# A graph network's weight tables: part of the low-weight multiplication moved from VectorE to GpSimd

## The reference

```
src, dst = sorted by dst                        # 103125 edges
# layer 0, ten times
agg = segment_sum((h * norm_src)[src], dst)     # counts of edges
h = 0.9 * (agg * norm_dst) + 0.1 * h0
# layer 1, three times, w = edge_weight
norm = dinv[src] * w * dinv[dst]
out = segment_sum((h @ W)[src] * norm, dst)     # weights of edges
```

## Time and profile before

| | |
|---|---|
| Median of three runs | 3808.62 us (3804.43 to 3809.42) |
| The profiled execution | 3773.04 us, span 3771.2 us |
| Mean granted TensorE clock over the span | 0.845 of full |
| PE busy over the span | 2851.2 us, 76% |
| DVE | 1979.1 us, 52% |
| ACT | 1593.7 us, 42% |
| POOL | 1698.0 us, 45% |

### The profile page before, as it was taken

The page is one execution under the profiler, slowest core; times in us unless marked ns, Lnnn a source line. Parts: engine busy times, 40 slices in busy tenths (PEclk is TensorE's granted clock), DMA queues, the critical chain, the costliest instruction groups (busy, mean ns, idle before and its releaser), DMA issues. The chain is left out here.

```text
span 3771.2 us, 69211 instructions
## 1 busy us (share of the span) xinstructions
PE 2851.2 (76%) x17480; PEld 1934.9 (51%) x17480; DVE 1979.1 (52%) x6941; ACT 1593.7 (42%) x4621; POOL 1698.0 (45%) x1766
## 2 busy tenths in 40 slices
PE   2777777999968857777777777778857777777778
PEld 2666654555534425566656566657734443434436
DVE  6999985666631444444444444446844444444443
ACT  1888871333300013333333333334634444444446
POOL 2222211444400046666666666663056666766660
PEclk6999999999989967777787877778868888889885
DMA  1222222556699922222222222222022222222220
GB/s 32 89 90 90 90 82 67 188 196 205 209 380 381 366 65 54 56 55 56 55 55 56 56 55 56 55 57 51 21 58 65 64 65 65 68 64 66 64 61 17
DMA packets 417669, 369.96 MB, mean 98 GB/s; under 512 B 175609, under 2 KB 342233, under 8 KB 417337
## 3 DMA queue, kind: packets, MB, share of 16 engines
q1 hardware_dynamic: 365912, 315.65, 25.7%
q0 software_dynamic: 46144, 48.98, 6.7%
q10 hardware_dynamic: 5280, 1.23, 0.1%
HBM read 279.65 MB, written 86.00 MB: 97 GB/s over the span
## 5 line engine op out<-in xcount | busy, mean ns | idle before, releaser
L1469 POOL DMA_INDIRECT big<-row_table,src x806 | 762.6, 946 | 459.1 <-issue 186.5
L1888 POOL DMA_INDIRECT big<-message_table,src x610 | 623.8, 1023 | 378.6 <-issue 167.8
L1494 PE MATMUL banks<-big 97*128 x902 | 398.1, 532 | 287.1 <-issue 269.2
L1576 DVE SCALAR_TENSOR_TENSOR big<-big,banks 128x97 f32 x451 | 142.6, 316 | 531.1 <-PE banks L1510 292.8
L505 PE MATMUL banks<-work 128*128 128x226 f16 x1197 | 312.3, 261 | 105.1 <-ACT banks L536 43.6
L1927 PE MATMUL banks<-big 128*128 128x512 f16 x1225 | 378.6, 425 | 5.1 <-DVE big L2006 5.1
L1510 PE MATMUL banks<-big 128*128 x1804 | 336.7, 320 | 38.6 <-issue 26.0
L869 PE MATMUL banks<-big,work 128*128 128x512 f16 (+1 forms) x1750 | 345.5, 355 | 17.0 <-DVE work L1006 17.0
L1521 ACT COPY big<-banks 97x256 f32<-97x256 f32 x403 | 148.1, 368 | 486.6 <-remote 270.0
L1494 PEld LDWEIGHTS banks<-big 97*128 97x128 f32 x902 | 173.4, 239 | 343.8 <-issue 339.8
L1510 PEld LDWEIGHTS banks<-big 128*128 128x128 f32 x1804 | 309.9, 243 | 49.7 <-issue 48.9
(11 more groups left out here) (339 smaller groups left out, 5701.2 us busy)
## 6 DMA issues: line engine op xcount, KB each, us to landing
big<-weights_halves SPq DMA_DIRECT2D x16, 6400.0 KB, 20.8
weights_dense<-work SPq DMA_DIRECT2D x196, 200.0 KB, 1.9
work<-weights_dense SPq DMA_DIRECT2D x196, 200.0 KB, 2.8
weights_halves<-work SPq DMA_DIRECT2D x98, 400.0 KB, 2.6
big<-q_table SPq DMA_DIRECT2D x451, 64.0 KB
big<-in_ef SPq DMA_DIRECT2D x403, 64.0 KB
big<-in_ea SPq DMA_DIRECT2D x403, 32.0 KB
big<-row_table,src POOLq DMA_INDIRECT x806
```

Of the source, the lines that this page charges most:

```text
L1469: po.indirect_dma_start(rows[:, t % RT, s, 0:D], None, x_t.rearrange("a p c -> (a p) c"), bass.IndirectOffsetOnAxis(ap=m.src2[:, s, t:t + ...
L1494: pe.matmul(psS[v % 2], qT[v % R][0:XW, :], XF[0:XW, bass.ds(slot, 1), :].rearrange("p t e -> p (t e)"), start=False, stop=True).then_inc( ...
L1888: po.indirect_dma_start(G[n % R][:, s, :], None, g_t.rearrange("a p c -> (a p) c"), bass.IndirectOffsetOnAxis(ap=m.src2[:, s, t:t + 1], ax ...
```

## The change

A new function `low_parts` on POOL multiplies the rows of the last four visits of a batch (LOWS = 6, so visits 6 to 9) by the low weights: 512 elements a partition. It waits until DVE has made the batch's rows (`rows_ready`) and adds one to a semaphore of its own, `lo_ready`. DVE multiplies only visits 0 to 5, 768 elements. PE waits for `lo_ready` before visit 6. POOL's copy for batch b waits for `lo_ready` of batch b - 2 besides, since it overwrites what that multiplication reads.

```diff
+        lo_ready = sem("build_lo")
...
+        LOWS = TP - 4
+        pairwise = lambda a: a.rearrange("p t (r u) -> p t r u", u=2)
+
+        def low_parts(po, b):
+
+            rows = slots[b % 2][0]
+            po.wait_ge(rows_ready, b + 1)
+            value = twice[b % 2][:, WLO, LOWS:TP, :].unsqueeze(2).to_broadcast([P, TP - LOWS, P // 2, 2])
+            po.tensor_tensor(pairwise(rows[:, 2, LOWS:TP, :]), pairwise(rows[:, 0, LOWS:TP, :]), value, ALU.mult).then_inc(lo_ready, 1)
+
         @block.gpsimd
         def _(po):
             for b in range(NBATCH):
                 if b >= 2:
                     po.wait_ge(oh_ready, b - 1)
+                    po.wait_ge(lo_ready, b - 1)
                 po.tensor_copy(twice[b % 2], m.tabs5()[:, :, b * TP:(b + 1) * TP].unsqueeze(3).to_broadcast([P, 5, TP, 2])).then_inc(doubled, 1)
+                if b >= 1:
+                    low_parts(po, b - 1)
+            low_parts(po, NBATCH - 1)
...
                 dve.wait_ge(rows_ready, b + 1)
-                for i, kind in ((1, WHI), (2, WLO)):
-                    ins = dve.tensor_tensor(pairwise(rows[:, i, :, :]), pairwise(rows[:, 0, :, :]), value(kind, P), ALU.mult)
-                ins.then_inc(oh_ready, 1)
+                dve.tensor_tensor(pairwise(rows[:, 1, :, :]), pairwise(rows[:, 0, :, :]), value(WHI, P), ALU.mult)
+                low = twice[k][:, WLO, 0:LOWS, :].unsqueeze(2).to_broadcast([P, LOWS, P // 2, 2])
+                dve.tensor_tensor(pairwise(rows[:, 2, 0:LOWS, :]), pairwise(rows[:, 0, 0:LOWS, :]), low, ALU.mult).then_inc(oh_ready, 1)
...
                 for t in range(min(TP, V0 - b * TP)):
+                    if t == LOWS:
+                        pe.wait_ge(lo_ready, b + 1)
                     if t % GV == 0:
                         pe.wait_ge(freed, needed[t // GV] & 255)
```

## The result

The changed kernel takes 3852.59 us (median of four runs, 3841.55 to 3858.78) against 3806.52 us (four runs, 3802.95 to 3809.42): ratio 1.0116, 95% interval [1.0101, 1.0132], 46 us slower. The forecast was 3889 us, slower, in a range from 3840 to 3945. The direction and the mechanism of steps 1 to 3 came as forecast; the size is a little over half of the 80 us, and the mechanism of step 4 did not occur.

The account below looks back on a forecast made before the run. PE, at 3.80 us a batch, bounds the table stage, with DVE close behind at 3.52. 119 x (4.45 - 3.80) = 77 us plus 3 us once gives 3808.6 + 80 = 3889 us; own range 3865 to 3915, outer 3840 to 3945.

Parts of the forecast that it names:

- steps 1 to 3: Table stage: DVE saves 0.27 us a batch, POOL's 1.19 us multiplication holds DVE 1.0 us; DVE's batch becomes 4.32 us.
- step 4: Table stage: POOL's multiplication doesn't get in until PE and DVE stop; 4.48 us a batch, up to 4.58; 4.45 taken.
- Step 1: DVE's second multiplication in the table stage loses 512 of 1280 elements: 0.27 us less, DVE's own work 3.25 us a batch.
- Steps 2 and 3: POOL's added table-stage multiplication takes 1.19 us a batch and, getting in ahead of L468, costs DVE 1.0 us.
- step 3: Table stage: POOL's multiplication holds DVE for 1.0 us a batch, its 1.19 us less 0.20.
- The sign that I had named: In the new profile's table stage, the last start of L481, the former L466, near 617 us.
- Step 6: Start of the table stage: POOL's configuration instruction ahead of its first multiplication costs 3 us once, between 0 and 8.
- Rival A: PE's clock falls in the table stage too: 0.35 us a batch more, 42 us, 3931 us; chance 0.17.
- Rival B: Table stage: POOL holds DVE only for elements read, at the copy's rate; 3.68 us a batch, 3809 us; chance 0.06.
- Rival C: Table stage: POOL and DVE run side by side, PE's sequencer ends the gain at 12 us, 3797 us; chance 0.05.
- Rival D: Table stage: DVE is stopped only 0.6 to 0.8 us a batch, about 30 us, 3839 us; chance 0.06.

Follow-up runs that it names:

- the saving alone: Changed kernel with the low weights of the last four visits multiplied by nobody from the third batch on: 3394.65 us against 3406.93 before; with one-batch legs 3403.74 us.
- the memset: Changed kernel with POOL setting the same 512 elements to zero instead of multiplying them: 3395.34 us against 3407.66 before, ratio 0.9965.
- before with legs of one: Kernel before, with PE reading 12 registers ahead of each batch instead of 24 ahead of every second: 3405.01 us against 3407.66, ratio 0.9990.

## Why the prediction was right

**What bounds the stage.** Right for the direction: DVE and PE both near 3.8 us, DVE with something to spare. Wrong in one point that didn't reach the sum: I took the pace of before as the larger of two numbers, 3.52 with small waits and 3.80. The table shows a blend, with PE's floor at 3.72. Above 4 us the blend is gone, so the distance to 4.17 us was not hurt by it.

**Step 1, the saving.** 0.27 us a batch predicted, 0.735 - 0.46 = 0.27 measured.

**Steps 2 and 3, the price.** The mechanism was right and was read from the right rows: two instructions that read SBUF take turns, and POOL gets in ahead of L468. The size was off. The multiplication lasts 1.03 us alone, not 1.19, because it costs 1.67 ns an element and not the 2.18 ns of the operations in the earlier trace rows. Those have f32 operands; no run shows whether that is the reason. Taking off 0.20 us for the start was right (0.18 us), so the hold is 0.85 us, not 1.0.

**Step 4, the form in which POOL is shut out.** This is the term whose mechanism did not come. I took DVE's 16 waits for POOL in the earlier trace rows for its count and let it pull the batch from 4.32 to 4.45 us. The count was read wrongly: of the 120 copies of before only ten take over 3 us, and others of those waits stand beside a copy of 0.27 us that ran while DVE was idle already (the wait at 193.28 us, with a copy at 192.89, is one). POOL was not shut out in one of the 118 batches: the longest multiplication is 1.992 us, 1.03 plus the wait for L482. In the traces a copy was shut out for a whole batch in before (3.59 us) and in three kernels in which POOL likewise reads nothing but its copies (the saving alone with either leg, and the memset, 3.32 us in each); in all the kernels in which POOL also multiplies or copies rows, and in before with legs of one, the longest copy is under 1 us. What decides it stays open; the moment of asking alone does not, since in the earlier trace rows the copy that was shut out and the one that got in both asked about 0.15 us after the start of an L466. My price of step 4, 4.48 us, was thus never tested.

**The sum.** With the two terms as measured, 3.25 + 0.85 + 0.07 = 4.17 us, (4.17 - 3.80) x 119 = 44 us, and 3 us once: 47 us, against 46 and 47 measured. Of the 33 us too much, 119 x 0.15 = 18 us come from step 3, the larger part, and 119 x 0.13 = 15 us from step 4. The sign that I had named, the last L481 near 617 us, was missed for the same reason (582.7 us); L483 over 1 us and POOL's multiplication far over 1.2 us in the median (1.99) came.

**Step 6, once.** 3 us predicted, 2.85 us of PE and 3.1 us of DVE measured; the configuration lay 7.0 us ahead.

**Rival A, the clock.** Out: 1.00 from 100 to 500 us, at a PE share of 281.64 / 400 = 70%. The stretch at 69% and 0.80 in the earlier trace rows was no guide to this stage. With eight visits on POOL, at 4.8 us a batch, the same stretch has PE busy for 64% and a clock of 0.97; there too the stage is the sum of DVE's steps and its waits at the start.

**Rival B** had the right sign of its doubt: its price per element read, 0.07 us for 100, is close to what was found, 0.08. It missed that a multiplication reads two operands. 512 x 2 x 0.7 ns would have been 0.72 us. This was the better way to the number than the duration of a different operation.

**Rival C** gave 12 us for the saving at no price, which is what the two kernels with legs of two gained in which POOL reads nothing but its copies. Its premise was wrong, its ceiling right.

**Rival D**, a hold of 0.6 to 0.8 us and 30 us in all, lay as near to the result as the forecast's own range did from the other side. I gave it 0.06, and the range from 3865 to 3915 us missed the result by 12 us; only the outer range held it, and only because it reached down to D. That the time lay inside is as much the width of that range as the sum.

## What to carry to other kernels

Before moving work from DVE to POOL, look for one POOL instruction beside DVE's two-input ones in the trace: if it lasts longer there than alone, count the elements that POOL would read, take the price of each from the neighbour's stretched duration, and compare with what DVE saves on an element. Here it was 1.66 ns against 0.52, so none of the splits run here won, and where DVE sets the pace each element moved loses. Only the work that POOL wrote without reading was free. Where two engines of nearly the same pace pass work through two slots and one of them has an uneven load, a small addition to the other need not be hidden: here 0.2 us a batch on DVE, under PE's pace, cost 8 us.

## What the runs showed of the hardware that was not expected

- A DVE instruction with two SBUF operands was held 0.81 ns for each element that a POOL instruction read: 0.41 us for one operand of 512 and 0.85 us for two. All operands were f16. A POOL memset of 512 elements beside them held it not at all.
- The hold is shown in the duration of the DVE instruction that starts next: a compare of 260 elements, 0.28 us by itself, showed 1.98 us.
- PE's load of registers from SBUF took 0.86 us for 12 and 1.85 us for 24, with the array idle. Half as many at a time, twice as often, left the stage's length within 1.3 us.
- The granted clock stayed at 1.00 with PE busy for 70% of the time and waits of up to 2.0 us for DVE, from 100 to 500 us of the changed kernel.
